# Windowed attention before a transformer block: the weighted sum over nine cells, on VectorE or inside TensorE's transpose

## What is computed

```python
pe  = conv(pixels, conv_w)                       # one row of 256 per cell
red = grid.mean(axis=(3, 5))                     # mean over a window's 9 cells
q   = _ln(red, ...) @ la_wq
kv  = _ln(win, ...) @ la_wkv                     # k and v of each cell
attn = softmax(einsum('bhnd,bhnkd->bhnk', q * scale, k_))   # over the 9 cells
agg  = einsum('bhnk,bhnkd->bhnd', attn, v_)      # weighted sum over the 9 cells
local_out = red + agg @ la_proj_w + la_proj_b
patch_out = local_out @ mod_w + mod_b            # the window tokens
```

## Time and profile before

| | before |
|---|---|
| median of 3 runs | 766.26 us |
| the profiled execution | 761.81 us |
| its span in the profile | 760.1 us |
| mean granted TensorE clock | 0.96 of 2.4 GHz |
| TensorE busy (matmul) | 690.5 us, 91% |
| VectorE busy | 535.0 us, 70% |
| GpSimd busy | 422.3 us, 56% |
| ScalarE busy | 394.8 us, 52% |
| the chain that ended last | TensorE 75%, VectorE 12%, DMA 4%, ScalarE 3%, GpSimd 2% |

### The profile page before, as it was taken

The page is one execution under the profiler, slowest core; times in us unless marked ns, Lnnn a source line. Parts: engine busy times, 40 slices in busy tenths (PEclk is TensorE's granted clock), DMA queues, the critical chain, the costliest instruction groups (busy, mean ns, idle before and its releaser), DMA issues.

```text
span 760.1 us, 23650 instructions
## 1 busy us (share of the span) xinstructions
PE 690.5 (91%) x9239; PEld 550.9 (72%) x9239; DVE 535.0 (70%) x1208; ACT 394.8 (52%) x969; POOL 422.3 (56%) x450
## 2 busy tenths in 40 slices
PE   5998969989987288999999999999999999999873
PEld 3987847778874166778778877878887887887651
DVE  2468585686877457678878878878878878866632
ACT  4563432634542145666666666666566566565431
POOL 3667371483643755475575575575675675663221
PEclk9999988999998589999999999999999999999997
DMA  9950470532220022222332332232232232122100
GB/s 221 237 143 1 119 222 1 145 77 47 62 60 22 19 58 69 76 64 67 79 74 74 77 80 72 77 78 74 74 77 76 73 77 78 39 61 57 35 20 25
DMA packets 69524, 58.69 MB, mean 77 GB/s; under 512 B 30607, under 2 KB 68646, under 8 KB 69286
## 3 DMA queue, kind: packets, MB, share of 16 engines
q1 hardware_dynamic: 69414, 57.18, 29.3%
HBM read 33.69 MB, written 11.40 MB: 59 GB/s over the span
## 4 chain that ended last, share of the span: by engine, by line
PE 75%; DVE 12%; DMA 4%; issue 3%; ACT 3%; POOL 2%; SPq 1%; POOLq 0%; DVEq 0%; ACTq 0%
PE p_a L1309 13%; PE p_c L1309 13%; PE p_s L1369 6%; PE p_conv L764 6%; PE p_o L1381 6%; PE p_kv L764 6%; PE p_n L1389 4%; PE p_c L1429 4%; PE p_s L1351 4%; PE p_a L1335 3%; PE p_s L1365 2%; PE p_mm L764 2%; PE p_c L1410 2%; DMA h<-h_tokens 2%; PE p_n L1395 2%
## 5 line engine op out<-in xcount | busy, mean ns | idle before, releaser
L1244 DVE TENSOR_REDUCE mx<-p_s 87x16 bf16<-87x1392 f32 x64 | 101.6, 1587 | 23.5 <-PE p_s L1351 23.4
L1104 POOL TENSOR_TENSOR t<-t,ss_rs 116x512 f32<-116x512 f32 x48 | 50.9, 1060 | 118.3 <-ACT ss_rs L1151 117.1
L1175 ACT ACTIVATE prT<-p_s 87x1392 f32<-87x1392 f32 x64 | 85.1, 1329 | 58.9 <-PE p_s L1369 57.4
L426 POOL TENSOR_TENSOR xs_lo<-xcols,xs_hi 120x585 fp32r<-120x585 f32 (+1 forms) x45 | 60.5, 1351 | 56.9 <-ACT xs_hi L489 56.9
L1100 POOL TENSOR_TENSOR t<-t 116x512 f32<-116x512 f32 x48 | 61.1, 1274 | 22.9 <-DVE t L1235 22.9
L1369 PE MATMUL p_s<-qr,kr 32*87 32x87 f32 x2048 | 68.4, 256 | 0.0
L1107 POOL TENSOR_TENSOR t<-t,tabs 116x512 f32<-116x512 f32 x48 | 63.0, 1312 | 3.8
L1309 PE MATMUL p_c<-w_f,yT 128*116 128x296 f32 x192 | 58.2, 426 | 2.0 <-ACT yT L1194 0.9
L1369 PEld LDWEIGHTS p_s<-qr,kr 32*87 32x87 f32 x2048 | 60.0, 153 | 0.0
L1365 PE MATMUL p_s<-mxT,pick_row 32*87 32x87 bf16 x1024 | 55.6, 207 | 1.4 <-ACT mxT L1169 1.4
L1381 PE MATMUL p_o<-prT,vp 87*32 87x87 f32 x2048 | 54.7, 246 | 0.0
(11 more groups left out here) (248 smaller groups left out, 1892.5 us busy)
## 6 DMA issues: line engine op xcount, KB each, us to landing
xcols<-in_x_cols SPq DMA_DIRECT2D x12, 822.7 KB, 12.1
h<-h_tokens SPq DMA_DIRECT2D x16, 348.0 KB
out<-out_sb SPq DMA_DIRECT2D x48, 116.0 KB
h_tokens<-in_txt SPq DMA_DIRECT2D x4, 1232.0 KB, 11.7
x<-in_txt_cols SPq DMA_DIRECT2D x32, 154.0 KB, 2.7
qr<-qkT SPq DMA_DIRECT2D x64, 58.0 KB, 2.0
kr<-qkT SPq DMA_DIRECT2D x64, 58.0 KB, 2.0
vp<-vt SPq DMA_DIRECT2D x32, 87.0 KB
```

What stands on the lines that cost most here:

```text
L426: nc.gpsimd.tensor_tensor(xs.lo[:, n % XS_SLOTS, :, 0:M].bitcast(F32R), raw, xs.hi[:, n % XS_SLOTS, :, 0:M], ALU.subtract).then_inc(S['xs_ ...
L1104: link(nc.gpsimd.tensor_tensor(t4, t4, ss_rs[:, b].unsqueeze(2).broadcast_to([TP, 2 * HEADS, HD]), ALU.mult))
L1175: nc.scalar.activation(prT[:, k % 2], p_s[0:SEQ, :, 0:QUADS * SEQ], ACT.Exp, scale=HD ** -0.5).then_inc(S['s_exp'], 1)
L1244: nc.vector.reduce_max(mx[:, k % 2, :, 0:QUADS], p_s[0:SEQ, :, 0:QUADS * SP].rearrange("p j (a k) -> p j a k", k=SP)[:, :, :, 0:SEQ], AX_X ...
```

## The change

The step `sum` goes, and with it `agg`, `agg_2`, their semaphore and the two entries of VectorE's table. In `aggT` TensorE makes the transposed sum itself: for each half of 128 value columns it multiplies the nine weighted cells as stationary operands with the identity as the moving one, all into the same place of `p_T`, and as a tenth product adds the bias, one row of `bias_kv` against a row of ones. It waits for the third `vw` of the step. Those that waited for `agg` now wait for `aggT`, the semaphore that these products raise. `CELLS` is 9, `CC` 2, `PIECES` and `LOAD_CELLS` 3.

```diff
-                score.2.498 s_max.0.517 att.0.538 sum.0.593 sum.1.638 lo.0.695 lo_var.0.700 patch.0.730 gv.0.752
+                score.2.498 s_max.0.517 att.0.538 lo.0.695 lo_var.0.700 patch.0.730 gv.0.752
...
-        agg, agg_2, aggT = sb("agg", [P, C]), sb("agg_2", [P, C]), sb("aggT", [P, CC, STEP_W])
+        aggT = sb("aggT", [P, CC, STEP_W])
...
                     if k % LOAD_CELLS == 0:
-                        wait(act, S['agg'], (n // LOAD_CELLS - KV_SLOTS) // PIECES + 1)
+                        wait(act, S['aggT'], (n // LOAD_CELLS - KV_SLOTS) // PIECES + 1)
...
-                if name == 'sum':
-                    cells = kv[0:M, ring(s, 0):ring(s, 0) + PIECES, :, C:2 * C].rearrange("p j n c -> p c (j n)")
-                    dve.wait_ge(S['vw'], PIECES * s + k + 2)
-                    if k == 0:
-                        wait(dve, S['aggT'], s)
-                        link(nc.vector.reduce_sum(agg[0:M], cells[:, :, 0:2 * LOAD_CELLS], AX_X))
-                        link(nc.vector.tensor_tensor(agg[0:M], agg[0:M], bias_kv[0:M, C:2 * C], ALU.add))
-                    if k == 1:
-                        link(nc.vector.reduce_sum(agg_2[0:M], cells[:, :, 2 * LOAD_CELLS:], AX_X))
-                        nc.vector.tensor_tensor(agg[0:M], agg[0:M], agg_2[0:M], ALU.add).then_inc(S['agg'], 1)
...
                 if name == 'aggT':
                     use('T', S['aggT_out'], s + 1)
-                    pe_.wait_ge(S['agg'], s + 1)
-                    transpose(p_T, agg[0:M], M).then_inc(S['aggT'], 1)
+                    pe_.wait_ge(S['vw'], PIECES * (s + 1))
+                    for c in range(CC):
+                        part = slice(C + P * c, C + P * (c + 1))
+                        mm_ = mm(p_T[:, c, 0:M], [kv[0:M, ring(s, j), i, part] for j in range(PIECES) for i in range(LOAD_CELLS)]
+                                 + [bias_kv[0:1, part]], [ident[0:M, 0:M]] * CELLS + [consts.ones[0:1, 0:M]])
+                    mm_.then_inc(S['aggT'], 1)
...
-                        pool.wait_ge(W['agg'], STEPS)
+                        pool.wait_ge(W['aggT'], STEPS)
...
-                        act.wait_ge(W['agg'], STEPS)
+                        act.wait_ge(W['aggT'], STEPS)
```

More of the change, by code:

```diff
@@ L337, in patch_tokens @@
                  "xs_hi xs_lo conv pe_out stat rstd xT xT_out xT_lo kv_mm kv_out red red_var red_rs redT redT_out q_mm q_ok q_kb "
-                 "prod score s_max s_exp att vw agg aggT aggT_out proj redb lo lo_var lo_rs loT loT_out mod patch patT patT_out "
+                 "prod score s_max s_exp att vw aggT aggT_out proj redb lo lo_var lo_rs loT loT_out mod patch patT patT_out "
                  "gv_mm gv gT g_m g_exp g_att gB gw ga ga_out cl cls_ok").split()
```

## The result

The kernel after takes 794.95 us (median of four runs, 793.46 to 795.83) against 765.83 us for the kernel before on the same chip (764.44 to 767.36). The ratio is 1.0378, with a 95% interval of 1.0351 to 1.0404: 29.1 us slower. The forecast was 785.9 us with a range of 777 to 793; the direction was right, and the loss is half as large again as the 19.6 us of the sum.

The account below looks back on a forecast made before the run. The prediction took TensorE's stream, without idle time ahead of the first three steps' transposes, to bound the kernel. Its terms 13.2 + 3.9 + 2.5 = 19.6 us on the median 766.3 gave 785.9 us, range 777 to 793.

Parts of the forecast that it names:

- What bounds the kernel: Whole kernel: TensorE's work ahead of about 264 us is mostly paid in full, and a stage that TensorE fills follows.
- steps 0 to 2: First three window steps: TensorE has no idle time before the transposes, so 3 x 4.4 = 13.2 us, all on the path.
- VectorE's freed time: Five sums, 23.9 us of VectorE: worth zero in the first three steps, then 0.49 us and 1.0 us.
- step 3: Fourth window step: TensorE had waited 0.49 us for the sum, so 4.4 - 0.49 = 3.9 us slower.
- The block, 40 x 0.115 = 4.6 us: Each step's added products: 40 MATMULs at 0.115 us, 4.6 us, less 0.2 us of transposes, 4.4 us net.
- A pace per record, not per column: Added products: the weight load sets the pace at 0.115 us a record, against 0.10 us for streaming 117 columns.
- rival (b): Added products are cheap, 0.084 us each by the kv products' streaming pace: 14 us slower, 780 us; chance 0.12.
- Step 4, net 2.5 us: Last window step: 22 slow records, 18 fast, result 5.5 us later; about 3.0 us come back as the clock rises sooner.
- Rival (e): Last window step: products cost as forecast but the clock rises no sooner, 24 us slower, 790.4 us; chance 0.13.
- Moved waits: Waits moved from `agg` to `aggT` and the wait for the third `vw`: no cost beyond the summed terms.
- (B): Theory set against the main one when experiments were planned: extra loss comes from beside the instructions, as moved waits or `p_T` held longer.

Follow-up runs that it names:

- e6_no_sum: Kernel after with two transposes of the first weighted cell in place of the 20 products, so no sum on either engine: 762.5 us, ratio 0.997 to the kernel before.
- e3_last_by_dve: Kernel after with VectorE's sum and the two transposes put back in the last step only: 785.71 us, ratio 1.0256 to the kernel before.
- e8_one_record: Kernel after with cell products in the rounded fp32 type, one record each, the last three cells summed three times: 782.58 us, ratio 1.0233 to the kernel before.
- e4_last_by_pe: Kernel before with the twenty products in the last step alone: 776.0 us, ratio 1.0136 to the kernel before.
- e9_warm_after: Kernel after with 28 useless wide products in TensorE's idle stretch ahead of the last step's rope transposes: 788.74 us, ratio 1.0306 to the kernel before.
- e2_tall_bias: Kernel after with the bias product made as high as a cell, 117 rows: 793.72 us, ratio 1.0359 to the kernel before.
- e5_both: Kernel before plus the twenty products, overwritten by the old transposes of VectorE's sum: 797.02 us, ratio 1.0428 to the kernel before.
- e11_narrow_before: Kernel before with 28 useless narrow fp32 products (56 records) ahead of the last step's rope transposes: 766.14 us, ratio 1.0003 to the kernel before.

## Why the prediction was right in direction and too small

**What bounds the kernel: right.** TensorE had no idle time ahead of the blocks of steps 0 to 2, and the chain has all five in full.

**VectorE's freed time: right.** Forecast 1.5 us in all, and `e6_no_sum` gives 2.9 with an interval of 0.2 to 4.5. At step 3 the delay is 4.33 us where the others have 4.75 to 5.06: the 0.49 us of the earlier trace rows came back.

**The block, 40 x 0.115 = 4.6 us: a term mis-sized.** The pace of a record was right (0.117; 4.39 us for 40 tall ones). The fault is that the bias product was counted as a record like the others: its four records cost 1.16 us and not 0.46, while the other 36 take 3.94 us where the forecast had 4.14. All 40 take 5.10 us. Less the 0.2 of the transposes that is 4.9 against 4.4, over four steps 19.04 against 17.1 at the copy, and by time 19.3 in `e3_last_by_dve`. The prediction did bound unknown rows from both sides, but took the bias under "128 stationary and 117 moving columns", and no row of before has one partition. The bound was there to draw: nothing in the trace excluded a dearer record.

**A pace per record, not per column: right, and that it is the weight load is argued.** `e8_one_record` halves the cell records and their time with them. In the rounded type 118 columns would stream in about 0.053 us by the pace of the kv products that the prediction's rival (b) uses, and a record still took 0.116, as did the 13-column records of the earlier trace rows. So the stream doesn't set it; a fixed cost of a record other than its load isn't excluded. The records follow each other at 110 to 117 ns. The Trainium skill, "TensorE: Matmul & The Clock Gate", gives about 81 ns at 128 moving columns in its section "Back-to-back issue gap", which did not hold for these records. By its section "LDWEIGHTS (loading the stationary operand)" a load of 128 columns takes an estimated 107 ns, the column count over 1.2, which came close.

**Step 4, net 2.5 us: the step that failed.** The prediction let the clock rise 5.5 us after the restart, as it had after an earlier pause, charged 22 slow records and 18 fast ones, and then took 3.0 us back, since what follows would be fast. Measured, all 40 records are slow: the copy comes 7.22 us later of this step's own, where 5.5 were forecast. And nothing came back: from the copy to the landing of `kr` another 2.6 us were lost, because `mod` and `gv` too, fast in the kernel before, were now slow. The first is 1.7 us and the second 2.6 + 3.0 = 5.6 us off, together 7.3; with the 1.9 of the early steps that is 9.2 of the 9.5 us by which the loss of 29.1 exceeds the sum of 19.6. `e4_last_by_pe` gives 9.6 us for this step by time, and `e9_warm_after` shows that the clock is what makes it.

The row that was carried over was also misread. At that pause of 3.67 us the clock hadn't yet fallen when TensorE restarted at 235.46; it fell 0.3 us later and was back at 239.2, 3.7 us after the restart and not 5.5. In stages of before (columns as in the earlier trace rows):

```profile
236.00:238.80 2.80, 2.80 (x7) 1.71 (x7) 2.58 (x4) 0.73 (x3) 1.46 (x3) 0.50 0.00 0
...
239.20:239.40 0.20, 0.20 (x2) 0.10 (x1) 0.00 (x0) 0.20 (x1) 0.20 (x1) 1.00 0.00 0
```

The row that should have been weighed is in the earlier trace rows itself: at 266.07, 6.7 us after the same restart, the qk product still had its slow 1.20 us. The trace of before thus said at this very place that 5.5 us had been too few (the clock was back after 10.5, past the end of a block), and a row from another pause was carried over instead. A return almost that soon does occur (6.0 us in `e3_last_by_dve`), but in none of the seven kernels with a block here.

**Rival (e), the clock that does not rise sooner: it was this one, and too small.** It had the whole block slow, 7 us net in place of 2.5, 790.4 us. It lacked the dear bias, some 0.5 us at each early step and 0.8 at the last (from the block's start to `proj` 288.47 - 278.43 = 10.04 us, in `e2_tall_bias` 287.18 - 277.93 = 9.25), and that the clock could come back later than in the kernel before: after 25.7 us and not 10.5. This last is why the range ended at 793.0, 2 us too soon: (e) was the case that happened, and the range had no room above it.

**Moved waits: right.** The kv copies, the first `exp` and the first `hb` show no new wait, and `e5_both`, which also has a wait for VectorE's sum, never stands still for it. (B) has nothing left to explain: blocks and clock add up to the loss.

**Still open:** what decides when the granted clock returns after TensorE's pause. The returns seen lie between 6 and 26 us after the restart, later with a block than without one save in `e11_narrow_before`, and whether the block is the reason isn't shown. `e9_warm_after` came out in two groups 8 us apart, of which only one of the faster was profiled. That the four runs of after lie within 2.4 us of each other while those of `e2_tall_bias` and `e3_last_by_dve` scatter by 10 and 8 is not explained either.

## What to carry to other kernels

A sum that looks free "inside the transpose" is a run of weight loads: count its records (two for each fp32 product), price each at its load, add the thin ones apart, and put the whole on the path if TensorE is the engine that is never idle there. What the other engine is freed of counts only where someone waited for it, and leaving the work out altogether shows in one run the most that a move can gain. Where TensorE stands idle for microseconds ahead of a place, charge everything behind it at the low clock, for at least as long as the trace of that same place shows.

## What the runs showed of the hardware that was not expected

- A record with one row of weights costs more than one with 117: 0.2 us from start to start and 0.29 with its neighbours, against 0.11, at 2.4 GHz, with the same 128 weight and 117 moving columns.
- The granted clock's return after a pause at this one place varies from 6.0 to 25.7 us after the restart, in kernels that differ only in what is queued. It can also fall only after the restart (in before, 0.3 us after the one at 235.46). Small products do run at 2.4 GHz; a filler that ends 4.7 us before the work gains nothing, one that ends 2 us before it makes the block fast.
- A loss of clock at one place moved more time (9.6 us for the last block) than the same 40 records anywhere else (4.8).
